# Turned inputs, rstd applied as k, v and q leave PSUM, batch 0 in parts, and first maxima in q tiles 3 to 6, in a Trainium2 transformer layer

## What is computed

```
h = layernorm(x)
q = h @ Wq            # 1024 x 1024, 32 heads of 32
k, v = split(h @ Wkv) # 1024 x 64, one head for all
p = softmax(causal(q k' / sqrt(32) + slope * (pos_k - pos_q)))
x = x + (p v) @ Wo
w = (unpack(qweight) - zero) * scale    # [n, k], four codes in three words
x = x + layernorm(x) @ w' + bias
```

## Time and profile before

| | |
|---|---|
| three runs | 889.77, 891.34, 891.32 us (median 891.32) |
| the profiled execution | 891.1 us, span 889.3 us |
| mean granted clock of PE | 0.991 |
| busy | PE 850.5 us (96%), PEld 620.6, DVE 536.4, POOL 390.4, ACT 331.8 |
| DMA | 117.19 MB, mean 132 GB/s |
| projection | 0 to 257 us |
| attention | 257 to 573 us, the first output tile begun inside it |
| output projection and codes | to the end |

### The profile page before, as it was taken

One profiled execution on the slowest core, in us unless ns is written; L12 is line 12 of the kernel. 1 busy time (PEld: TensorE's weight loads), 2 busy tenths in 40 slices (PEclk: granted clock), 3 DMA queues, 4 the chain that ended last, 5 costly groups with the idle time before them and its releaser, 6 DMA issues.

```text
span 889.3 us, 13953 instructions
## 1 busy us (share of the span) xinstructions
PE 850.5 (96%) x4912; PEld 620.6 (70%) x4912; DVE 536.4 (60%) x1527; ACT 331.8 (37%) x647; POOL 390.4 (44%) x254
## 2 busy tenths in 40 slices
PE   2789999999989999999999999999999999999997
PEld 2578888888865555555555555578888888888885
DVE  6455253542575788888887777356655455555535
ACT  2323122222135767767766656422112112111211
POOL 1000000000016888888888888855443333444211
PEclk9989999999998999999999999999999999999999
DMA  5445554449443664666665572574344533334211
GB/s 160 145 157 154 166 160 145 138 133 219 137 119 89 154 150 124 153 145 142 147 150 154 157 182 76 156 187 119 96 117 130 127 100 107 95 95 117 73 48 48
DMA packets 90110, 117.19 MB, mean 132 GB/s; under 512 B 9060, under 2 KB 51044, under 8 KB 89960
## 3 DMA queue, kind: packets, MB, share of 16 engines
q1 hardware_dynamic: 90040, 116.30, 49.3%
HBM read 76.95 MB, written 38.93 MB: 130 GB/s over the span
## 4 chain that ended last, share of the span: by engine, by line
PE 89%; DVE 3%; DMA 3%; ACT 2%; SPq 1%; POOL 1%; issue 1%; DVEq 0%; ACTq 0%
PE p_o L529 19%; PE p_st L692 13%; PE p_s L677 10%; PE p_st L609 10%; PE p_o L677 9%; PE p_o L620 9%; PE p_s L582 9%; PE p_o L633 4%; PE p_st L529 2%; PE p_s L522 1%; DMA xt<-ml 1%; DMA raw<-in_wq_dram 1%; PE p_st L599 1%; PE p_s L706 1%; PE p_st L706 1%
## 5 line engine op out<-in xcount | busy, mean ns | idle before, releaser
L948 DVE CUSTOM_DVE_ANT_0 spill<-p_s,mask 128x128 bf16<-128x128 f32 (+3 forms) x512 | 224.2, 482 | 69.1 <-PE p_s L582 66.5
L439 POOL TENSOR_SCALAR_AFFINE_SELECT pt<-pt 128x512 f32<-128x512 f32 x128 | 83.1, 662 | 302.8 <-ACT pt L789 302.8
L789 ACT ACTIVATE pt<-p_st 128x512 f32<-128x512 f32 (+1 forms) x352 | 178.3, 560 | 90.5 <-PE p_st L609 90.2
L529 PE MATMUL p_o<-xt,wqh 128*128 128x512 f32 x512 | 170.1, 398 | 2.2 <-DVE wql L1058 2.2
L582 PE MATMUL p_s<-kst,xt 98*128 98x128 f32 (+3 forms) x512 | 149.7, 331 | 0.0
L609 PE MATMUL p_st<-xt,kst 100*128 100x512 f32 (+1 forms) x352 | 142.2, 408 | 6.1 <-DMA xt<-ml 4.6
L529 PEld LDWEIGHTS p_o<-xt,wqh 128*128 128x128 f32 x512 | 97.1, 190 | 22.8 <-DVE wql L1058 2.6
L446 POOL TENSOR_TENSOR pt<-pt 128x1536 f32<-128x1536 f32 x32 | 111.7, 3490 | 2.7
L582 PEld LDWEIGHTS p_s<-kst,xt 98*128 98x128 f32 x512 | 99.5, 195 | 11.9 <-DVE mx L948 0.9
L529 PE MATMUL p_o<-xt,wql 128*128 128x512 f32 x256 | 100.5, 392 | 0.0
L609 PEld LDWEIGHTS p_st<-xt,kst 100*128 100x128 f32 x352 | 66.9, 191 | 43.2 <-DVE ml L955 18.3
(11 more groups left out here) (104 smaller groups left out, 1205.1 us busy)
## 6 DMA issues: line engine op xcount, KB each, us to landing
xt<-qh_d SPq DMA_DIRECT2D x64, 256.0 KB
xin<-in_x_dram SPq DMA_DIRECT2D x16, 512.0 KB, 3.9
qh_d<-qh SPq DMA_DIRECT2D x32, 256.0 KB, 2.6
ql_d<-ql SPq DMA_DIRECT2D x32, 256.0 KB, 3.2
xt<-ql_d SPq DMA_DIRECT2D x32, 256.0 KB
o_d<-o_st SPq DMA_DIRECT2D x32, 256.0 KB, 2.8
ob<-o_d SPq DMA_DIRECT2D x64, 128.0 KB, 4.1
inv_b<-inv_d SPq DMA_DIRECT2D x64, 128.0 KB, 4.6
```

The costliest lines, as they stand in the source:

```text
L439: pool.affine_select(out=own, in_=own, compare_op=ALU.is_ge, fill=0.0, base=0, pattern=[[0, 4], [1, P]], channel_multiplier=-1).then_inc(c ...
L529: last = pe.matmul(dst, w[:, c, cols], xs[:, c, :], start=(c == 0 and k == 0), stop=(c == CK - 1 and k == 2))
L789: act.activation(pt[s % 2][:, j:j + heads, PT_AT[kb]:PT_AT[kb] + KB_LEN[kb]], p_st[:, place(k) % 3, 0:heads * KB_LEN[kb]].rearrange("p (j ...
L948: dve.tensor_tensor_reduce(spill[:, SPILL_AT[qb]:SPILL_AT[qb] + keys], scores_of(n), mask[:, S - keys:S], 1.0, LOWEST, ALU.add, ALU.max, m ...
```

## The change

x is given twice: in rows as before, for the statistics alone, and turned (x_t, features by rows). The features of x, wq, wkv, wo, the codes, scale, zero and bias are given in a permuted order (`feature_order`), so that each 128 of them come from the same position in the groups of four codes, and the codes are given turned. The host undoes the order in the output. On the chip:

- x_t chunks of 128 features x 512 rows (xs) are centred on DVE by the mean of each row, split by ACT and DVE, and used directly: PE turns no x and no codes. For batch 0 the mean is eight matmuls with a matrix of 1/1024; for the others it is read from the row statistics.
- The row statistics (mean and rstd, eight floats a partition) go to DRAM (st_d) and come back as rows broadcast to all partitions (`spread_stats`): rstd_b and mean_b.
- rstd is multiplied in as k, v and q leave PSUM, on DVE: kt by `keys_values`, q by `scaled_q` into qt, which frees the bank; then ACT copies qt into qh and DVE makes ql.
- Batch 0 goes feature part by feature part: for each part of 128 the k/v tile and q tiles 0 to 3 together, then tiles 4 to 7. q has five banks in batches 0 to 2 and two in the last. wq comes in 16 pieces of 256 KB through four buffers, the first four issued by ACT with the k/v weights.
- The eight code parts are unpacked one by one as 128 x 1024, in tiles 2 and 6 of each batch, no longer shifted by 32.
- In the last batch the first maxima stand in q tiles 3 to 6, and the maxima of steps 0 and 1 are both turned and stored before attention. In `attend(s)` SP stores the maxima of s + 1 before it issues the q load of s + 3.
- The last tile of `ffn` has banks of its own in p_s.

```diff
+        p_q = (p_o, p_sum, p_s[:, 0, :], p_s[:, 1, :], p_s[:, 2, :])
...
+        p_mean = p_st[:, 2, :]
...
+        p_ff = [p_st[:, 0:2, :]] * (TILES - 1) + [p_s[:, 0:2, :]]
...
+        STATS = {0: (0, 1), 1: (2,), 2: (3,)}
+        CENTRE = {4: (0, 1), 5: (2, 3), 6: (4, 5), 7: (6, 7)}
+        UNPACK = {2: 0, 6: 1}
+        EARLY = {3: 0, 4: 8, 5: 16, 6: 24}
...
+        def bank(n):
+            return n % 5 if n < CK * LASTB else n % 2
...
+            def load_xs(b, c):
+                at_least(sp, x_lo, CK * (b - 1) + c + 1)
+                sp.dma_start(xs[:, c, :], xt_v[:, c, b * S:(b + 1) * S]).then_inc(xs_in[c], 16)
+            def spread_stats(b):
+                sp.wait_ge(ln_rstd, 2 * TPB * (b + 1))
+                sp.dma_start(st_v[b], mr[:, b % 2, :], allow_slow_non_contiguous=True).then_inc(st_out, 16)
+                sp.wait_ge(st_out, 16 * (b + 1))
+                at_least(sp, q_freed, CK * (b - 1))
+                at_least(sp, kt_done, 2 * (b - 1))
+                sp.dma_start(rstd_b[:, b % 2, :], st_d[b:b + 1, S:2 * S].to_broadcast([P, S])).then_inc(rstd_in, 16)
+                if b > 0:
+                    at_least(sp, x_mid, CK * b if b > 1 else 0)
+                    sp.dma_start(mean_b[:, :], st_d[b:b + 1, 0:S].to_broadcast([P, S])).then_inc(mean_in, 16)
...
             def project(b):
                 more = b < LASTB
                 if more:
+                    if b > 0:
+                        load_x(4 * b + 4)
+                        load_x(4 * b + 5)
+                        for c in range(CK):
+                            load_xs(b + 1, c)
+                    load_codes(2 * b)
+                    load_x(4 * b + 6)
+                    load_x(4 * b + 7)
+                else:
+                    load_codes(2 * b)
                     sp.wait_ge(q_done, CK * LASTB)
                     for s in range(3):
                         load_q(s)
                 for m in range(CK):
+                    if not more and m in (6, 7):
+                        store_max(m - 6)
                     n = CK * b + m
-                    sp.wait_ge(q_freed, n + 3)
                     rows, cols = slice(m * P, (m + 1) * P), slice(b * S, (b + 1) * S)
+                    sp.wait_ge(qh_done, n + 1)
                     sp.dma_start(qh_d[rows, cols], qh[:, m % 2, :].bitcast(F32)).then_inc(q_out[m % 2], 16)
+                    sp.wait_ge(ql_done, n + 1)
                     sp.dma_start(ql_d[rows, cols], ql[:, m % 2, :].bitcast(F32)).then_inc(q_out[m % 2], 16)
+                    if more and m == 2:
+                        spread_stats(b + 1)
+                    if m in UNPACK:
+                        e = 2 * b + UNPACK[m]
+                        sp.wait_ge(wt_done, e + 1)
+                        sp.dma_start(wi_d[:, e, :], wt[:, :].bitcast(F32)).then_inc(wt_out, 16)
+                        if UNPACK[m] == 0:
+                            load_codes(e + 1)
...
             def attend(s):
+                if 0 < s < STEPS - 1:
+                    store_max(s + 1)
                 if s + 3 < STEPS:
                     at_least(sp, st_done, NU * s)
                     load_q(s + 3)
-                if s + 1 < STEPS:
-                    store_max(s + 1)
                 if s > 0:
...
+            for c in range(CK):
+                load_xs(0, c)
+            load_x(0)
+            load_x(1)
+            sp.dma_start(kt[R_BIAS:R_END, :], kpos).then_inc(kpos_in, 16)
             sp.dma_start(ext_d, slopes.rearrange("r h s -> r (h s)")).then_inc(ext_out, 16)
+            load_wq(4)
+            load_x(2)
+            load_wq(5)
+            load_x(3)
+            for u in (6, 7, 8):
                 load_wq(u)
+            load_x(4)
+            load_x(5)
+            load_wq(9)
+            spread_stats(0)
+            for u in range(10, 2 * CK):
+                load_wq(u)
+            for c in range(CK):
+                load_xs(1, c)
...
+            def mean():
+                pe.wait_ge(consts, 6)
+                for c in range(CK):
+                    pe.wait_ge(xs_in[c], 16)
+                    last = pe.matmul(p_mean, share[:, :], xs[:, c, :], start=(c == 0), stop=(c == CK - 1))
+                last.then_inc(mean_done, 1)
...
+            def queries(b, m, c):
+                n = CK * b + m
+                if c == 0:
+                    at_least(pe, q_freed, bank_before(n) + 1)
+                if b == 0:
+                    pe.wait_ge(wq_lo, CK * (m // 4) + c + 1)
+                last = chunk(p_q[bank(n)], wqh, wql, slice(m * P, (m + 1) * P), b, c)
+                if c == CK - 1:
+                    last.then_inc(q_done, 1)
...
+            def project(b):
+                together = 4 if b == 0 else 0
                 for c in range(CK):
+                    keys_values(b, c)
+                    for m in range(together):
+                        queries(b, m, c)
+                for m in range(together, CK):
                     for c in range(CK):
+                        queries(b, m, c)
+                        if b == LASTB and m in EARLY:
                             score(EARLY[m] + c)
+                        if b == LASTB and (m, c) == (6, 0):
+                            turn_max(0)
+                        if b == LASTB and (m, c) == (7, 2):
+                            turn_max(1)
+                    if m == (5 if b == 0 else 0):
+                        turn_v(b)
...
+                if t < TILES - 1:
+                    at_least(pe, scaled, t)
+                else:
+                    pe.wait_ge(x2_done, TILES - 1)
...
+            def x_high(b, c):
+                act.wait_ge(x_mid, CK * b + c + 1)
+                if c == 0:
+                    at_least(act, q_done, CK * (b - 1))
+                act.copy(xt(b, 0)[:, c, :], xs[:, c, :]).then_inc(x_hi, 1)
...
+                    if more:
+                        for t in STATS.get(m, ()):
+                            std(4 * b + 4 + t)
+                        for c in CENTRE.get(m, ()):
+                            x_high(b + 1, c)
+                    if not more and m in (6, 7):
+                        max_high(m - 6)
+                    if m in UNPACK:
+                        e = 2 * b + UNPACK[m]
+                        act.wait_ge(unpacked, e + 1)
+                        at_least(act, wt_out, 16 * e)
+                        act.copy(wt[:, :], qi[:, :]).then_inc(wt_done, 1)
...
+            def centre(b, c):
+                dve.wait_ge(xs_in[c], 16 * (b + 1))
+                if b == 0:
+                    dve.wait_ge(mean_done, 1)
+                else:
+                    dve.wait_ge(mean_in, 16 * b)
+                dve.tensor_tensor(xs[:, c, :], xs[:, c, :], p_mean if b == 0 else mean_b[:, :], ALU.subtract).then_inc(x_mid, 1)
+            def x_low(b, c):
+                dve.wait_ge(x_hi, CK * b + c + 1)
+                dve.tensor_tensor(xt(b, 1)[:, c, :], xs[:, c, :], xt(b, 0)[:, c, :], ALU.subtract).then_inc(x_lo, 1)
...
+            def scaled_q(n):
+                b, m = n // CK, n % CK
+                dve.wait_ge(q_done, n + 1)
+                dve.wait_ge(rstd_in, 16 * (b + 1))
+                at_least(dve, ql_done, n - 1)
+                dve.tensor_tensor(qt[:, m % 2, :], p_q[bank(n)], rstd_b[:, b % 2, :], ALU.mult).then_inc(q_freed, 1)
+            def q_low(n):
+                b, m = n // CK, n % CK
+                dve.wait_ge(qh_done, n + 1)
+                at_least(dve, q_out[m % 2], 32 * (n // 2))
+                dve.tensor_tensor(ql[:, m % 2, :], qt[:, m % 2, :], qh[:, m % 2, :], ALU.subtract).then_inc(ql_done, 1)
+            def project(b):
+                more = b < LASTB
                 for m in range(CK):
                     n = CK * b + m
+                    if more:
+                        for t in STATS.get(m, ()):
+                            moments(4 * b + 4 + t)
+                    if m == 0:
+                        keys_values(b)
+                    if more:
+                        for t in STATS.get(m, ()):
+                            rstd(4 * b + 4 + t)
+                        for c in CENTRE.get(m, ()):
+                            centre(b + 1, c)
+                            if c > 0:
+                                x_low(b + 1, c - 1)
+                    if m in UNPACK:
+                        unpack(2 * b + UNPACK[m])
+                    if not more and m == 7:
+                        max_low(1)
                     if not more and m in EARLY:
                         for i in range(CK):
                             maximum(EARLY[m] + i)
+                            if m == 6 and i == 2:
                                 max_low(0)
+                    scaled_q(n)
+                    q_low(n)
+                if more:
+                    x_low(b + 1, CK - 1)
...
+            centre(0, 0)
+            for c in range(CK):
+                if c + 1 < CK:
+                    centre(0, c + 1)
+                x_low(0, c)
```

(93 more changed lines are left out.)

299 lines of the change are left out of this document (101 added, 198 removed).

## The result

The changed kernel takes 1002.2 us (median; 987.9 to 1003.2), the kernel before on the same chip 890.6 (889.5 to 891.3): ratio 1.120, 95% interval 1.108 to 1.132. The side was right; the size was wrong, 105 us off. The profiled execution took 1001.9 us, its span 1000.1.

The account below looks back on a forecast made before the run. The prediction took PE (TensorE), busy 850.5 of 889.3 us, as the bound. From 891.1 us it took 18.7 of gains and added 25 for the late q load: forecast 897 us, own range 892 to 911, 8 in 10 in 876 to 913.

Parts of the forecast that it names:

- the q load behind the maxima store: Attention: the later q load sets the step if it lands in over 4.86 us; 0.9 us a step, 25 us lost.
- Batches of 49.7 us: Steady projection batches: without x and code turns, k/v tiles of batches 2 and 3 stand 49.7 us apart, before 54.24.
- The tail's 2.2: Last tile of the tail: other banks remove PE's 2.17 us wait before 877.64, a gain of 2.2 us.
- The gains without the two troubles, 18.7 us: Sum of gains over batch 0, steady batches, attention's start, a late wait and the tail: 18.7 us.
- the landing L of 5.8: Attention's q load: 1.8 us of a small transfer plus 0.803 MB at 202 GB/s, landing in 5.8 us.
- the bound of 35: Attention: upper end of the range kept for the late q load's loss, 10 to 35 us around 25.
- Rival 1: First score of each attention step: q lands in time or nearly, below 5.4 us, so the change is faster; chance 0.30.
- No stall, with 1 us to spare: Steady batches: the mean returns 11 us after q tile 2; x_low ready at 31 us, PE wants it at 32.
- Rival 2: Projection: statistics' store takes 8 us or more; batch 0 ends 4 later, batches 1 and 2 lose 2 each; 905 us; chance 0.08.
- PE starts at 18.7: Batch 0: DVE copies kpos before the first centre, so PE starts at 18.7 us, not 25.33.
- 4.2 less, I take 4.0: Attention's start: two steps' maxima done beforehand, step 0 takes 8.5 and step 1 9.6 us; gain taken as 4.0.
- The wait of 1.08 at 530.39 goes too: Late attention: PE's wait of 1.08 us at 530.39 disappears, a gain of 1.1 us.

Follow-up runs that it names:

- Experiment 2: Kernel before with one swap alone: SP issues the maxima rows ahead of the q load in each attention step; 985.5 us, ratio 1.105.
- experiment 11: Kernel before with maxima rows issued ahead of the q load, and a third of that load left out from step 4 on; 912.0 us, ratio 1.024.
- experiment 5: Changed kernel, q load again ahead of maxima, statistics spread by PE, next batch's x rows loaded and reduced earlier, DVE's list reordered; 872.8 us, ratio 0.978.
- experiment 3: Changed kernel, q load again ahead of maxima, statistics not stored and broadcasts reading rows of x instead; 877.5 us, ratio 0.982.
- experiment 9: Kernel before with maxima rows ahead of the q load, and two zero-weight matmuls filling PE's idle time in 25 steps; 969.2 us, ratio 1.087.
- experiment 1: Changed kernel with the order put back: q loads issued ahead of the maxima rows in each attention step; 914.7 us against 893.5, ratio 1.024.
- experiment 4: Changed kernel, q load again ahead of maxima, mean and rstd spread by PE matmuls without store or broadcasts; 881.9 us, ratio 0.988.
- experiment 6: Changed kernel, q load ahead of maxima, statistics spread by PE, x rows early, and batch 0 going tile by tile; 874.2 us, ratio 0.980.
- experiment 10: Kernel before with maxima rows ahead of the q load, and SP waiting for q rows to land before other transfers; 965.6 us, ratio 1.081.

## Why the prediction was wrong

**Right.** The mechanism that decides was named with its place: the q load behind the maxima store, PE idle before the step's first score, 28 or 29 times, in a loop that closes on itself. Experiment 2 shows it alone and experiment 11 shows its arithmetic. Batches of 49.7 us come out at 51.3 with 1.8 of spreading in them once PE waits little (experiment 5). The tail's 2.2 came (2.8 behind the last turned score).

The gains without the two troubles, 18.7 us, are 16.0 in experiment 3, but the nearness of the totals is in part luck. In the two traces 9.5 us are gained before attention (the sum has 11.4), 2.2 in it (5.1) and 2.8 behind it (2.2).

**Failed: the landing L of 5.8, "The steady row is the nearest: 0.9 us a step, in 28 steps (loads of s = 1 to 28) 25 us".** It cost 86 to 92 us. The step of the prediction is the landing, and behind it a part that was missing:
- L was built as "the 1.8 of a small transfer and the bytes over a rate". Measured 6.95. The rate (202) was near (185). The fixed part was 2.6, not 1.8. That q is four transfers that SP issues one behind another, the last 1.51 us after the first (347.50 to 349.01), is the likely reason; no run issued them otherwise, so it is argued and not shown. DMA moved by microseconds from 347.50 on, same columns as the windows above:

```profile
347.50:348.50 1.00, 1.00 (x19) 0.56 (x17) 0.92 (x5) 0.65 (x2) 0.00 (x0) 1.00 0.05 11
348.50:349.50 1.00, 1.00 (x13) 0.89 (x6) 1.00 (x4) 0.45 (x2) 0.00 (x0) 1.00 0.54 137
349.50:350.50 1.00, 1.00 (x12) 0.52 (x14) 1.00 (x5) 1.00 (x4) 0.51 (x1) 1.00 0.82 158
350.50:351.50 1.00, 1.00 (x17) 0.50 (x10) 0.58 (x6) 0.45 (x1) 0.92 (x2) 1.00 0.87 203
```

  With this alone the step is 2.82 + 6.95 + 1.89 = 11.7 and the loss 28 x 2.1 = 59 us: outside the bound of 35 that the prediction kept.
- The trace of before held a nearer number. In it nobody waits for this load, so the page prints no landing, but the events of its semaphore put the last part 7.3 to 9.0 us after the first issue (median 7.8; 20 steps, 300 to 500 us), with a store of o and a load of wo issued just ahead. The issue at 299.11 had until 308.96, 9.85 us. Put in the loop, 7.8 makes steps of 12.5 us.
- Nothing in the sum let the gap change the clock. The prediction had charged 1.5 us of clock in the head and read a fall of the clock behind the 3.47 us wait, yet gave the 28 new gaps none. With gaps near 2 us in every step the turn-to-issue term grows by 0.33 and the score-to-turn term by 0.82; where the clock is 0.97 to 0.99 (experiments 9 and 11) they stay at 2.81 and 1.84. 28 x 1.15 = 32, and 59 + 32 = 91, near the 86 to 92 measured.

The Trainium skill's page "DMA: Bandwidth & Descriptors", section "Anatomy of one DMA", would have it shorter still, by an estimate 3.3 us for the 0.549 MB that took 5.58 here; its figures are for one transfer issued by GpSimd, and these are four issued by SP. Rival 1, with its chance of 0.30, fell: from 300 to 500 us no run landed the 0.80 MB in under 6.4 us.

**Failed: the statistics' trip, "No stall, with 1 us to spare".** The store was taken at 5.0, "the nearest load in the same stage", with bounds 1.8 to 10; it takes 9.0 to 9.3, inside the bounds and near their end. The mean's broadcast takes 5.5 to 5.7, not 3.7. mean_in comes about 15 us after the store's issue, against 8.7 in the sum, and the sum had 1 us to spare. Rival 2 ("8 us or more") was the true case, but priced 4 + 2 x 2 us: it holds some 37 (experiment 3). It missed that the delay feeds itself: x_low late makes the xs loads of the next batch late, the x rows stand behind those (landing 8.66 us at 117.24), the next statistics leave later, and the last wq pieces stand behind the store in the head.

The Trainium skill's page "DMA: Bandwidth & Descriptors", section "Rules for kernel authors", says that a last dimension that isn't contiguous becomes one descriptor for each element. The trace agrees: between the store's issue at 77.35 and its landing it has 1057 packets under 512 bytes (DMA's busy share of that stretch in 40 slices):

```profile
DMA  0099897720000000000000000000000000000000
DMA packets 1190, 0.28 MB, mean 31 GB/s; under 512 B 1057, under 2 KB 1057, under 8 KB 1190
```

These lines say more than that: the packets are through 2 us after the issue, and for the 7 us until the landing is told the DMA engines move nothing. What fills these 7 us isn't shown. 8 KB of maxima land in 1.8, but no run stored the same 4 KB in another form, so that the single floats make it slow is argued, not shown.

**Failed in the head:** "PE starts at 18.7": 20.58, since kpos landed at 16.84, ahead of the first centre on DVE. Experiment 5 moved that copy behind: 17.97.

**Failed at attention's start:** "4.2 less, I take 4.0" and "The wait of 1.08 at 530.39 goes too". The 3.47 is gone, but PE waits 2.23 us for ACT's exponentials ahead of it (0.89 before), and the late wait for the maxima row is still there. In experiment 1:

```profile
286.40 0.79 PE L659 MATMUL p_st<-xt,kst 100*128 100x512 f32 x1 [2.23 <-ACT pt L840]
...
555.07 0.50 PE L659 MATMUL p_st<-xt,kst 100*128 100x512 f32 x1 [1.66 <-DMA xt<-ml]
```

In the traces of experiments 1, 3, 4, 5 and 6 attention takes 310.6 to 314.8 us, before 314.3: between nothing and 3.7 of the 5.1 counted.

## What to carry to other kernels

When a load is moved later in a queue, add up its loop from rows, with every issue of a transfer in several parts as a term, and take the landing from the first issue to the last byte, from the events of the load's own semaphore where the trace has them. If the loop comes out longer than the step, charge the engine's clock too: here gaps near 2 us in every step cost more than their length, and gaps of 0.2 to 0.6 us did not. And before a tile of statistics goes to DRAM in single elements, see whether PE can spread it, a column repeated as weights against the identity: 1.8 us a batch here for a trip of 15.

## What was not expected of the hardware

- Gaps of 0.2 to 0.6 us in each step leave the granted clock at 0.99 (experiment 11); gaps of about 2 us in steps of 13 bring it to 0.91 on the mean, and eight matmuls behind a gap take 1.94 us for 1.06. Two matmuls of zeros in the gap bring it back to 0.97 and the kernel 16 us forward.
- A store of 1024 single floats from 128 partitions takes 9.0 to 9.3 us, of which the DMA engines work for some 1.3, and the queue behind it stands still for that time, because SP waits for it.
- A landing 0.3 us shorter went with 20 us (experiment 10). The term behind the gap fell by 0.6 us with it; that the shorter gap keeps the clock up in more steps fits this, but no run separates the two.
